# Moving TensorE's work around two waits: router and first expert products inside the last routed branch, the second refine layer ahead of x1's transposes

## The reference, cut to what matters

```python
logits = gelu(xf @ router_w1 + router_b1) @ router_w2 + router_b2
topk_p, topk_i = top_k(softmax(logits), 2)          # two experts for each row
integrated, v = xf, zeros
for _ in range(2):                                   # stage 1, stage 2
    ctx = concatenate([integrated, v])
    shared_ctrl = gelu(ctx @ shared_w1 + b) @ shared_w2 + b
    ctrl = gelu(ctx @ expert_w1[e] + b) @ expert_w2[e] + b   # for both chosen e
    x_next, v_next = weighted mix of inl(shared_ctrl) and inl(ctrl) for both e
    halt = sigmoid(gelu(integrated @ halt_w1 + b) @ halt_w2 + b)
    integrated, v = integrated + halt*(x_next-integrated), v + halt*(v_next-v)
refined = gelu(integrated @ refine_w1 + b) @ refine_w2 + b
out = xf + integration_weight * refined
```

## Time and profile before

| | |
|---|---|
| median of 3 runs | 964.01 us (958.92 to 969.05) |
| profiled execution, its own time | 960.8 us |
| its span | 959.0 us |
| TensorE busy, weight loads busy | 802.6 us, 665.7 us |
| VectorE, ScalarE, GpSimd busy | 693.3, 554.3, 302.6 us |
| mean granted TensorE clock | 0.932 of full speed (2.4 GHz) |

### The profile page before, as it was taken

The page is one execution under the profiler, slowest core; times in us unless marked ns, Lnnn a source line. Parts: engine busy times, 40 slices in busy tenths (PEclk is TensorE's granted clock), DMA queues, the critical chain, the costliest instruction groups (busy, mean ns, idle before and its releaser), DMA issues.

```text
span 959.0 us, 14857 instructions
## 1 busy us (share of the span) xinstructions
PE 802.6 (84%) x4784; PEld 665.7 (69%) x4784; DVE 693.3 (72%) x1708; ACT 554.3 (58%) x1392; POOL 302.6 (32%) x393
## 2 busy tenths in 40 slices
PE   4578888888888898888888888888888988988875
PEld 2457677776777687777777777767776776776764
DVE  3846778768678678687787686687787787786743
ACT  7355475465565655654754655656656556556555
POOL 1523234225133233333343242242332332333111
PEclk7569999999999999999999999999999999999896
DMA  8000000000000000000000000000000000000000
GB/s 323 0 6 6 6 1 12 1 12 12 1 12 12 1 12 12 1 12 11 2 12 10 3 12 1 12 12 1 12 12 1 11 8 0 7 7 0 6 7 12
DMA packets 7709, 14.40 MB, mean 15 GB/s; under 512 B 792, under 2 KB 6864, under 8 KB 7248
## 3 DMA queue, kind: packets, MB, share of 16 engines
q1 hardware_dynamic: 7632, 13.45, 3.9%
HBM read 10.30 MB, written 3.15 MB: 14 GB/s over the span
## 4 chain that ended last, share of the span: by engine, by line
DVE 46%; PE 27%; issue 15%; ACT 7%; POOL 5%; DMA 0%; POOLq 0%; DVEq 0%; ACTq 0%
PE ctl L434 7%; DVE hm_hi L928 6%; DVE work L967 6%; DVE work L1003 3%; PE ctl L443 3%; DVE gl L942 3%; PE pa L412 3%; DVE work L965 2%; DVE xf L1061 2%; ACT mexp L743 2%; POOL rs L376 2%; DVE work L1030 2%; DVE holo L1025 2%; PE pb L412 2%; ACT gh L720 2%
## 5 line engine op out<-in xcount | busy, mean ns | idle before, releaser
L335 POOL TENSOR_TENSOR hm_lo<-gl,mexp 128x256 fp32r<-128x256 f32 x144 | 121.5, 863 | 388.2 <-DVE gl L942 388.2
L434 PE MATMUL ctl<-w2e_hi,hm_hi 128*128 128x512 f32 (+1 forms) x432 | 170.1, 401 | 3.1 <-DVE hm_hi L928 1.7
L434 PE MATMUL ctl<-w2e_lo,hm_hi 128*128 128x512 f32 (+1 forms) x432 | 159.2, 380 | 0.0
L928 DVE TENSOR_TENSOR hm_hi<-ge,mexp 128x256 fp32r<-128x256 f32 x144 | 89.6, 632 | 48.6 <-ACT mexp L743 38.6
L443 PE MATMUL ctl<-w2e_hi,hm_lo 128*128 128x512 f32 (+1 forms) x432 | 112.7, 380 | 3.0
L434 PEld LDWEIGHTS ctl<-w2e_hi,hm_hi 128*128 128x128 f32 x432 | 87.8, 203 | 26.2 <-DVE hm_hi L928 14.9
L443 PEld LDWEIGHTS ctl<-w2e_hi,hm_lo 128*128 128x128 f32 x432 | 77.9, 202 | 33.7 <-POOL hm_lo L335 20.4
L713 ACT ACTIVATE ge<-pa,par 128x128 f32<-128x128 f32 x192 | 53.7, 355 | 81.8 <-PE pa L412 81.8
L434 PEld LDWEIGHTS ctl<-w2e_lo,hm_hi 128*128 128x128 f32 x432 | 88.6, 205 | 11.4
L731 ACT ACTIVATE work<-ctl 128x256 f32<-128x256 f32 (+1 forms) x144 | 68.9, 479 | 38.8 <-PE ctl L446 38.8
L412 PE MATMUL pa<-x1T,par 128*128 128x128 f32 x768 | 89.7, 275 | 0.0
(11 more groups left out here) (175 smaller groups left out, 1838.2 us busy)
## 6 DMA issues: line engine op xcount, KB each, us to landing
out_dram<-y SPq DMA_DIRECT2D x24, 128.0 KB, 1.7
work<-params_dram SPq DMA_DIRECT2D x1, 2560.0 KB, 10.4
xa<-x_dram SPq DMA_DIRECT2D x16, 128.0 KB, 2.3
work<-params_dram SPq DMA_DIRECT2D x1, 1664.0 KB, 13.9
par<-params_dram SPq DMA_DIRECT2D x1, 1280.0 KB, 16.5
xa<-x_dram SPq DMA_DIRECT2D x8, 119.0 KB
par<-params_dram SPq DMA_DIRECT2D x1, 530.5 KB, 4.6
work<-params_dram SPq DMA_DIRECT2D x1, 512.0 KB, 3.6
```

The costliest lines, as they stand in the source:

```text
L335: TT(hm[1][:, j, c, :], gl[:, c, :], pairs(tile, j, c), ALU.mult).then_inc(done, 1)
L434: mm(dst[:, a:z], hm[0][:, j, c, :], w2e[i][:, c, a:z], start=(c == 0 and i == 0), stop=False)
L928: V.tensor_tensor(hm[0][:, j, c, :], ge[:, c, :], pairs(tile, j, c), ALU.mult).then_inc(done, 1)
```

## The change

`expert_control` is cut into three functions, `expert_hi` (L434's products for one span), `expert_end` (L437) and `expert_lo` (L443, L446). Calls of `expert_control` elsewhere do the same in the same order. For the last routed branch of stage 2 the three are called one by one, and TensorE's order in a slot becomes: `expert_hi` for the first 512 columns; the transposes of `xf`; `expert_hi` for the other 256 columns and `expert_end`; the router's, shared and first expert chunk's hidden products and the logits; `expert_lo`; `x2`'s transposes; the experts' other chunks; the mask's transposes; both chunks of the first refine layer's first half. The second refine layer's block (`if o.exists()`) moves ahead of the transposes of `x1`. On ScalarE `shared_units` for `f` moves ahead of x2T and of the last branch's `unit`. The instructions are the same in kind and number. SyncE, GpSimd and VectorE are unchanged.

```diff
-            def expert_control(dst, j, tile, hi_v, end_v, lo_g, end_sb, done, ncols):
-
-                spans = [(a, min(ncols, a + 512)) for a in range(0, ncols, 512)]
+            def spans(ncols):
+
+                return [(a, min(ncols, a + 512)) for a in range(0, ncols, 512)]
+
+            def expert_hi(dst, j, tile, hi_v, a, z):
+
+                for c in range(PC):
+                    if j == 0 and a == 0 and c == 2:
+                        passed(pe, hi_v, tile, per=3, step=2)
+                    for i in range(2):
+                        mm(dst[:, a:z], hm[0][:, j, c, :], w2e[i][:, c, a:z], start=(c == 0 and i == 0), stop=False)
+
+            def expert_end(dst, j, tile, end_v, ncols):
+
+                passed(pe, end_v, tile, per=2, step=j + 1)
+                for a, z in spans(ncols):
+                    mm(dst[:, a:z], hm[0][:, j, PC, :], w2a[:, 1 + j, a:z], start=False, stop=False)
+
+            def expert_lo(dst, j, tile, lo_g, end_sb, done, ncols):
...
+            def expert_control(dst, j, tile, hi_v, end_v, lo_g, end_sb, done, ncols):
+
+                for a, z in spans(ncols):
+                    expert_hi(dst, j, tile, hi_v, a, z)
+                expert_end(dst, j, tile, end_v, ncols)
+                expert_lo(dst, j, tile, lo_g, end_sb, done, ncols)
...
+                if n.exists():
+                    passed(pe, hm2_v, n, per=3)
+                    passed(pe, u2_sb, n, per=BR, step=1)
+                    expert_hi(ctl[1], 1, n, hm2_v, 0, 512)
+
                 if f.exists():
                     passed(pe, xf_v, f)
                     for q in range(KD):
...
                 if n.exists():
-                    passed(pe, hm2_v, n, per=3)
-                    passed(pe, u2_sb, n, per=BR, step=1)
-                    expert_control(ctl[1], 1, n, hm2_v, en2_v, hl2_g, eb2_sb, u2_ps, 3 * D)
+                    expert_hi(ctl[1], 1, n, hm2_v, 512, 3 * D)
+                    expert_end(ctl[1], 1, n, en2_v, 3 * D)
 
                 if f.exists():
                     passed(pe, xfT_sb, f)
                     passed(pe, mv2_v, f)
                     hidden(pd, HID, w1r, range(1), xfT, KD, rh_ps)
+
+                    if f.low == 0:
+                        pe.wait_ge(par_in[1], 16)
...
+                    hidden(pb, P, w1s, range(1), xfT, KD, s1_ps)
...
+                    hidden(pa, P, w1e, range(1), xfT, KD)
+
+                    passed(pe, rh_sb, f)
+                    mm(pd[:, 0:E], rh[:, :], pv("w2r", HID), start=True, stop=True).then_inc(lg_ps, 1)
+
+                if n.exists():
+                    expert_lo(ctl[1], 1, n, hl2_g, eb2_sb, u2_ps, 3 * D)
 
                 if m.exists():
                     passed(pe, x2_v, m)
...
                 if m.exists():
-                    hidden(ctl[1][:, 512:1024], P, r1, range(1, EC // 2), x2T, KD)
+                    passed(pe, x2T_sb, m)
+                    if n.exists():
+                        passed(pe, u2_sb, n, per=BR)
+                    else:
+                        passed(pe, rg_sb, m, back=1)
+                    hidden(ctl[1][:, 512:1024], P, r1, range(EC // 2), x2T, KD)
```

More of the change, by code:

```diff
@@ L423, in shared_control @@
                 last.then_inc(done, 1)
-            def expert_control(dst, j, tile, hi_v, end_v, lo_g, end_sb, done, ncols):
-                spans = [(a, min(ncols, a + 512)) for a in range(0, ncols, 512)]
-                rows = MR if j == 0 else P
[L429 to L437, removed]
+            def spans(ncols):
[11 more added lines that the diff above has]
+            def expert_lo(dst, j, tile, lo_g, end_sb, done, ncols):
+                rows = MR if j == 0 else P
                 passed(pe, lo_g, tile, per=3, step=2 * j + 1)
-                for a, z in spans:
+                for a, z in spans(ncols):
                     for c in range(PC):
@@ L505, in slot @@
                     expert_control(ctl[0], 1, t, hm1_v, en1_v, hl1_g, eb1_sb, u1_ps, 2 * D)
+                if o.exists():
+                    passed(pe, rgl_g, o)
+                    passed(pe, y_v, o, back=1)
+                    for i, (part, w) in enumerate(((0, 0), (0, 1), (1, 0))):
+                        for c in range(REF // P):
+                            last = mm(refined, rgp[part][:, c, :], r2[w][:, c, :], start=(i == 0 and c == 0),
+                                      stop=(i == 2 and c == REF // P - 1))
+                    last.then_inc(rl2_ps, 1)
                 if n.exists():
@@ L518, in slot @@
                     last.then_inc(x1T_ps, 1)
[L520 to L527, removed]
                 if z.exists():
@@ L618, in slot @@
                     hidden(pd, HID, w1r, range(1), xfT, KD, rh_ps)
[L620 to L631, removed]
                     if f.low == 0:
@@ L648, in slot @@
                     mm(pd[:, 0:E], rh[:, :], pv("w2r", HID), start=True, stop=True).then_inc(lg_ps, 1)
-                    hidden(pa, P, w1e, range(1, EC), xfT, KD, e1_ps)
[L652 to L659, removed]
+                if n.exists():
+                    expert_lo(ctl[1], 1, n, hl2_g, eb2_sb, u2_ps, 3 * D)
+                if m.exists():
+                    passed(pe, x2_v, m)
+                    if f.exists():
+                        passed(pe, xfT_sb, f)
+                    elif n.exists():
+                        passed(pe, x1T_sb, n)
+                    else:
+                        passed(pe, x2T_sb, m, back=1)
+                    for q in range(KD):
+                        last = nc.tensor.transpose(pc[:, q * P:(q + 1) * P], x2[:, q * P:(q + 1) * P], ident)
+                    last.then_inc(x2T_ps, 1)
+                if f.exists():
+                    hidden(pa, P, w1e, range(1, EC), xfT, KD, e1_ps)
                     if f.low == 0:
@@ L838, in slot @@
                     AF(rh[:, :], pd[0:HID, 0:P], ACT.Gelu, bias=pv("b1r", HID)).then_inc(rh_sb, 1)
+                if f.exists():
+                    shared_units(f, s1_ps, s1_sb, sh1, sa1, sb1, halt1_ps, sl1_v)
                 if m.exists():
@@ L843, in slot @@
                     unit(n, 2, u2_sb, u2_ps, ctl[1], 3)
-                if f.exists():
-                    shared_units(f, s1_ps, s1_sb, sh1, sa1, sb1, halt1_ps, sl1_v)
                 if f.exists():
```

## The result

The changed kernel takes **986.1 us** (985.24 to 987.34, 4 runs) against 963.42 (958.92 to 969.05): a ratio of 1.0233, 95% interval 1.0177 to 1.0289.

What follows compares the result with a forecast made beforehand. VectorE was taken to lead the chain, with TensorE on it in places. Order +8, clock falls +5.4, tail 0 on 960.8 us gave 974.2, plus 1: 975; range 970 to 980, 8 in 10 within 958 to 984.

Steps and rivals of the forecast that it cites:

- Part 1: Ahead of the router: the 2.0 us wait for `xf` becomes about 2.4 us for xfT; router starts 0.3 us earlier.
- Part 2: From router to mask transposes on TensorE: 5.08 us instead of 4.41, so the mask's transposes come 0.36 us later.
- Part 3: Behind the mask: the mask expansion starts 0.35 us later, hidden by ScalarE's expert GELUs; taken as 0.
- Part 4: Refine layer ahead of `x1`'s transposes: fills TensorE's 1.95 us wait, worth 0 since the chain runs on VectorE there.
- Part 5: TensorE's clock behind the wait: falls in 20 of 22 slots at 1.25 us each, 25 us instead of 19.6, +5.4.
- A deeper loss: Every slot's fall costs 1.7 us and Part 3's 0.35 is not hidden: 994, with only one about 984; chance 0.11.
- Falls stay as frequent: TensorE's clock falls as often as before, so only 8 us are added: 969 to 972; chance 0.25.
- TensorE is the bound: TensorE's filled waits come back, mask 2.1 us earlier in 22 slots, if ScalarE's copy follows `xf` at once: 915; chance 0.05.
- The clock stops falling: Split and filled waits on TensorE end the falls, if the wait for xfT is under 2 us: 949; chance 0.09.

Runs made afterwards that it cites:

- copy_early: The changed kernel with ScalarE's xfT copy moved up, right behind the attention's exponential: 911.23 us, ratio 0.9488.
- wait_filled: The changed kernel with nine extra 512-column products, results thrown away, just before the wait for xfT: 942.16 us, ratio 0.9819.
- router_only: The changed kernel with the second refine layer put back behind `x1`'s transposes: 991.95 us, ratio 1.0318.
- wait_half_filled: The changed kernel with four extra 512-column products, results thrown away, just before the wait for xfT: 941.84 us, ratio 0.9864.
- scalar_old_order: The changed kernel with ScalarE's order put back, x2T copy and last branch's evacuation ahead of the shared units: 993.61 us, ratio 1.0343.
- before_filled: The kernel before with seven extra 512-column products, results thrown away, just before the wait for `xf`: 952.52 us, ratio 0.9953.
- hi_ahead_only: The kernel before with only the last routed branch's first 512-column span of high products ahead of `xf`'s transposes: 948.3 us, ratio 0.9921.
- hi_and_refine_ahead: The kernel before with the first span of high products ahead of `xf`'s transposes and the second refine layer ahead of `x1`'s: 929.29 us, ratio 0.9677.

## Why the prediction was right in kind and wrong in size

**Part 1 held.** The wait for xfT was forecast at 2.4 us and is 2.37, the one for `xf` at about 0.5 and is 0.61. The cover that was "gone" was the thing to see, and `copy_early` shows that this copy alone decides between 2.3% slower and 5.1% faster.

**Part 2 held.** 5.08 us from router to mask, 5.04 in `wait_filled`. Parts 1 to 3 forecast 0.36 a slot; the full-clock slot of this order is 36.18, so 0.23. The mask's transposes wait for nothing, as said.

**Part 3 held** in that no 0.35 appeared (ScalarE copies the first expanded mask 1.26 us behind `maskT`, 1.27 before), and ScalarE's move was rightly read as what keeps it from waiting: undone, it costs 7.5 us.

**Part 4 was right for a path that does not change its clock, and wrong otherwise.** VectorE's path gives nothing for it: 0.9995. But the reasoning missed a wait that matters through the clock alone: with the fall behind `xf` gone, the move is worth 15 and 19 us. That did not make the miss. In the changed order the move's net worth is not clear of zero, and a gain would go the other way.

**Part 5 is the step that failed: the falls' cost was mis-sized, 25 us forecast, 39.4 measured.** That is 20 slots of the changed kernel (763.1) less 20 of `wait_filled`, the same order without a fall (723.7). The frequency was right (20 of 22 forecast; in the trace every one of the 20 slots). The price was not. It was taken at 1.25 us a fall, "near the lower end", on the idea that part of it would pass under the wait. No row gives the bounds 1.1 and 1.7; the row at hand gave 1.44, and in the 12 slots of before with a fall at `xf` the low stretch begins 0.9 to 1.4 us behind the issue of `xf`'s transposes, so behind the wait. In 16 of the 20 slots of the changed kernel it begins 0.4 us or more behind the end of the wait and hits path work in full: 37.7 less 36.18 is 1.5. And in 7 of 20 the low stretch was twice as long, 39.0 less 36.18 or 2.8 us, which neither the trace of before nor any case of the prediction had. The doubles are the larger part of the miss (7 at 1.3 more make 9 us; 20 at 0.25 more make 5): with 1.44 for each fall the forecast would have been 979, within its range. The account for 20 slots: order 723.7 - 719.0 = 4.7, falls 39.4 - 19.6 = 19.8, together 24.5, as measured. Why some slots get the double stretch is not settled by these runs. In this trace it is those where it begins earliest, 3.7 to 5.5 us behind `xf` against 5.6 to 6.2 in the others; in `router_only` too the four doubles are the earliest.

**The rivals.** "A deeper loss" was nearest. With the full price alone it is 22 x (0.36 + 1.7) - 19.6 = 25.7, or 986.5, but the fit is partly luck: the mean fall cost 1.97 and the order 0.23, and the hidden 0.35 did not come. "Falls stay as frequent" is refuted by 20 of 20. "TensorE is the bound" is refuted by `wait_filled`: 200 more products, and no loss. Its condition, a copy that follows `xf` at once, is what `copy_early` brings, and 911 is close to its 915, yet not for its reason: about half of the gain over 20 slots (19.6 of 42.0 us) is the clock's. "The clock stops falling" asked for a wait under 2 us: with 1.44 left, `wait_half_filled` takes 942 where that case said 949. With the copy early the falls stop too, and the logits then come early as well.

## What to carry to other kernels

When a reorder takes work out from between a producer and its consumer, look up when the consumer's input is ready on every engine in between: here ScalarE's copy had 0.3 us of slack behind a 4 us block, and the block was all that hid it. On TensorE count waits by their length, those off the path too: a wait of 2 us cost nothing in itself and 1.4 to 1.5 us where the clock fell behind it, and removing one such wait brought the other's falls up. A few unused products in the wait tell in one run whether an order or the clock is to blame.

## What the runs showed of the hardware

- With a wait of 2.37 us in each slot TensorE ran at the 1.2 GHz level in part of every slot of the changed kernel and of `router_only`, and of 18 of 20 in `scalar_old_order`; with 1.44 (`wait_half_filled`) in none. Waits of 1.93 to 2.3 us are in between, and the length alone doesn't say how often: in the kernel before 12 of 20 behind `xf` and 1 of 20 at `x1`; at `x1` 4 of 20 in `router_only`, 8 in `before_filled`, 15 in `hi_ahead_only`.
- The low stretch can begin within the wait or behind it: in the changed kernel from 1.2 us before its end to 1.3 us after.
- Whether the number of falls makes the spread between runs is not shown, since each kernel has one trace. The kernel before spreads over 20 us (948.55 to 968.49 in 19 runs), four kernels of four runs each over less than 3 (941.22 to 944.03, 940.97 to 942.58, 893.47 to 894.91, 985.24 to 987.34). But `hi_and_refine_ahead`, with no fall in its 20 slots, spreads over 6.2, and `hi_ahead_only`, with 15, over 4.7 in ten runs.
- Product for product, work in a wait was free here: `wait_filled` and `wait_half_filled` differ by 0.3 us with five products a slot between them.
